# Attention and mixture of experts on one core: one transpose per group's shifts, the logits' maxima a step earlier, and small arithmetic of the norms on GpSimd

## What is computed

```python
mod = (silu(c) @ wmod).reshape(16, 6, 1, 128)          # sa, ca, ga, sb, cb, gb
h = layernorm(x, eps=1e-5) * (1 + ca) + sa
x = x + ga * attention(h)                              # 16 heads of 8, rope, causal
h = layernorm(x, eps=1e-5) * (1 + cb) + sb
x = x + gb * ffn(h)
# ffn: logits = h @ router.T; the 2 best of 8 experts per token;
#      shares = softmax over the two; out = sum of share * expert(h), hidden 512, gelu
```

## Time and profile before

| what | before |
|---|---|
| median of three runs | 526.88 us |
| the profiled execution, its own time | 525.71 us |
| its span, first to last instruction | 523.9 us |
| TensorE busy, share of the span | 455.6 us, 87% |
| VectorE busy | 385.0 us, 73% |
| ScalarE busy | 327.8 us, 63% |
| GpSimd busy | 329.0 us, 63% |
| granted TensorE clock, mean | 0.960 |

### The profile page before, as it was taken

One profiled execution on the slowest core, in us unless ns is written; L12 is line 12 of the kernel. 1 busy time (PEld: TensorE's weight loads), 2 busy tenths in 40 slices (PEclk: granted clock), 3 DMA queues, 4 the chain that ended last, 5 costly groups with the idle time before them and its releaser, 6 DMA issues.

```text
span 523.9 us, 12596 instructions
## 1 busy us (share of the span) xinstructions
PE 455.6 (87%) x3546; PEld 336.6 (64%) x3546; DVE 385.0 (73%) x1171; ACT 327.8 (63%) x896; POOL 329.0 (63%) x465
## 2 busy tenths in 40 slices
PE   4389999999999899989989999799789889999980
PEld 4255656665555555655656665389688788999970
DVE  4678898899999899999899899735336523434783
ACT  4666667656656556556566565677566557787860
POOL 3244465458858857957867958845656664444781
PEclk9689999999999999999999999899989789999995
DMA  4345655564664655664655862422212322223744
GB/s 120 101 129 150 135 152 152 140 182 140 184 177 135 180 143 162 195 175 126 188 135 146 172 155 80 132 73 64 72 52 66 88 73 67 69 67 106 226 135 140
DMA packets 77987, 67.88 MB, mean 130 GB/s; under 512 B 10916, under 2 KB 71592, under 8 KB 77921
## 3 DMA queue, kind: packets, MB, share of 16 engines
q1 hardware_dynamic: 71984, 57.18, 41.3%
q0 software_dynamic: 4320, 8.47, 5.0%
q10 hardware_dynamic: 1616, 1.44, 0.8%
HBM read 25.47 MB, written 12.05 MB: 72 GB/s over the span
## 4 chain that ended last, share of the span: by engine, by line
PE 38%; DVE 18%; issue 14%; POOL 13%; DMA 7%; ACT 5%; another core or an unknown queue 2%; SPq 2%; ACTq 1%; DVEq 0%; POOLq 0%
PE ps_sc L1637 8%; DVE maxima L1452 5%; PE ps_pv L1744 4%; PE misc L1627 4%; PE ps_max L1627 4%; PE misc L1790 4%; POOL sorted_rows L714 3%; POOL probs L764 3%; PE ps_sc L1715 3%; PE ps_max L1697 2%; POOL results L754 2%; DMA sorted_rows<-rows,slots 2%; ACT after_k L862 2%; PE ps_max L1618 1%
## 5 line engine op out<-in xcount | busy, mean ns | idle before, releaser
L1452 DVE TENSOR_REDUCE maxima<-ps_max 128x2 f32<-128x512 f32 (+1 forms) x192 | 130.1, 682 | 21.1 <-PE ps_max L1699 18.0
L930 ACT ACTIVATE probs<-ps_sc 128x512 f32<-128x512 f32 x192 | 109.8, 595 | 52.3 <-PE ps_sc L1715 40.8
L754 POOL DMA_INDIRECT results<-after_k,after_e x71 | 70.2, 988 | 63.5 <-DVE after_k L1149 46.0
L1715 PE MATMUL ps_sc<-q_diags,k_stacks 128*128 128x512 f32 x192 | 97.2, 508 | 5.7 <-ACT probs L930 3.3
L764 POOL TENSOR_SCALAR_AFFINE_SELECT probs<-probs 128x512 f32<-128x512 f32 x128 | 82.5, 652 | 24.5 <-ACT probs L930 23.2
L1637 PE MATMUL ps_sc<-wproj_s,after_k 128*128 x568 | 81.8, 289 | 1.8 <-ACT after_k L862 0.8
L1637 PEld LDWEIGHTS ps_sc<-wproj_s,after_k 128*128 128x128 f32 x568 | 72.2, 199 | 7.0 <-issue 4.7
L714 POOL DMA_INDIRECT sorted_rows<-rows,slots x64 | 65.4, 1021 | 14.5 <-issue 9.6
L1149 DVE SCALAR_TENSOR_TENSOR after_k<-ps_sc,after_e,after_k 128x128 f32<-128x128 f32 x71 | 24.8, 349 | 62.2 <-PE ps_sc L1637 32.3
L1697 PE MATMUL ps_max<-k_diags,q_stacks 128*128 128x512 f32 x128 | 61.2, 479 | 2.1 <-DVE maxima L1452 1.9
L1744 PE MATMUL ps_pv<-probs,v_wides 128*32 128x256 f32 (+1 forms) x1024 | 55.2, 333 | 3.6 <-POOL probs L764 3.5
(11 more groups left out here) (189 smaller groups left out, 920.8 us busy)
## 6 DMA issues: line engine op xcount, KB each, us to landing
k_diags<-k_stacks SPq DMA_DIRECT2D x64, 128.0 KB
q_diags<-q_stacks SPq DMA_DIRECT2D x64, 128.0 KB
gate_now<-gate_rows SPq DMA_DIRECT2D x16, 320.0 KB
after_e<-sorted_rows SPq DMA_DIRECT2D x71, 65.0 KB
k_stacks<-high SPq DMA_DIRECT2D x32, 128.0 KB
q_stacks<-high SPq DMA_DIRECT2D x30, 128.0 KB
x_in<-in_x SPq DMA_DIRECT2D x16, 128.0 KB, 2.8
k_stacks<-low SPq DMA_DIRECT2D x16, 128.0 KB
```

Source lines behind the costliest of these rows:

```text
L754: nc.gpsimd.indirect_dma_start(result_dram, bass.IndirectOffsetOnAxis(ap=row_in[m % RING][:, D + 1:D + 2].bitcast(U32), axis=0), y_out[m % ...
L930: nc.scalar.activation(probs[:, g % 2, c], ps_sc[u % 2][:], ACT.Exp, scale=SCALE).then_inc(S["exp_done"], 1)
L1452: nc.vector.tensor_reduce(to, of, AX, ALU.max).then_inc(S["max_done"], 1)
L1715: last = nc.tensor.matmul(ps_sc[u % 2][:].rearrange("p (w q) -> p w q", w=4), k_stack[(s.t + d) % 3][:, g, keys * P:(keys + 1) * P], q_dia ...
```

## The change

- **Shifts.** `shifts` now holds both query tiles side by side, 16 columns in the order part, head, tile. One transpose gives 16 rows of 128; ScalarE copies 16 x 128, and the DMA reads 16 rows of 128 in place of 8 rows of 256. 
- **Epsilon.** VectorE's 32 additions (L1050) go; GpSimd does them right ahead of its root, in slot 5 and slot 10. VectorE now waits ahead of the aggregation for the last reader of `moments`.
- **nmr.** VectorE's 14 instructions (L1546) go; GpSimd makes mean times rstd and then its negative behind the root in slot 10, each behind a wait for the one before, on 14 images.
- **Logits' maxima.** The four MAX8 of a routing step (slot 5) move to the end of the step before it (slot 11). The indices move from slot 7 to 5, `find_hot` from slot 8 to 7. The last pair of images, in the tile stage, stays as it was.
- The transpose of a bias in the prologue counts on another semaphore.

```diff
-        shifts = sb("shifts", [P, 2, TILES, P], F32R)
-        shift_t = [sb(f"shift_t{n}", [8, T], F32R) for n in range(2)]
+        shifts = sb("shifts", [P, 2, P], F32R)
+        shift_t = [sb(f"shift_t{n}", [8 * TILES, P], F32R) for n in range(2)]
...
                     if n == RESIDUAL_AT + 1 and s.has(-2):
+                        s.wait(pool, S["moments2_done"], -2, 2, 2)
+                        nc.gpsimd.tensor_scalar_add(var_eps2[:], moments2[:, :, 1], EPS).then_inc(S["eps2_done"], 1)
                         s.wait(pool, S["eps2_done"], -2, 1, 1)
...
                     if d and s.has(d):
+                        s.wait(pool, S["moments_done"], d, 2, 2)
+                        nc.gpsimd.tensor_scalar_add(var_eps[:], moments[:, :, 1], EPS).then_inc(S["eps_done"], 1)
                         s.wait(pool, S["eps_done"], d, 1, 1)
                         s.wait(pool, S["z_done"], d - 1, 2, 2)
                         nc.gpsimd.tensor_tensor(rstd[:], var_eps[:], half_s[:], ALU.pow).then_inc(S["rstd_done"], 1)
+                        if d == 3:
+                            s.wait(pool, S["rstd_done"], d, 1, 1)
+                            nc.gpsimd.tensor_tensor(var_eps[:], moments[:, :, 0], rstd[:], ALU.mult).then_inc(S["mean_scaled"], 1)
+                            s.wait(pool, S["mean_scaled"], 1, 1, 1)
+                            nc.gpsimd.tensor_scalar(nmr[:], var_eps[:], -1.0, None, ALU.mult).then_inc(S["nmr_done"], 1)
...
-                    nc.scalar.activation(shift_t[g % 2][:], misc[BANK[f"sh{g}"]][0:8, 0:T], ACT.Copy).then_inc(S["shift_out"], 1)
+                    nc.scalar.activation(shift_t[g % 2][:], misc[BANK[f"sh{g}"]][0:8 * TILES, 0:P], ACT.Copy).then_inc(S["shift_out"], 1)
...
                 s.wait(dve, S[sd], d, 2, 2)
+                s.wait(dve, S[rd], d - 1, 1, 1)
+                if d == 3 and s.t >= 0:
+                    dve.wait_ge(S["nmr_done"], s.t + 1)
                 for a in range(TILES):
                     nc.vector.bn_aggr(mo[:, a, :], st[:, a, :]).then_inc(S[md], 1)
-                s.wait(dve, S[md], d, 2, 2)
-                s.wait(dve, S[rd], d - 1, 1, 1)
-                nc.vector.tensor_scalar_add(ve[:], mo[:, :, 1], EPS).then_inc(S[ed], 1)
...
-                    v = shifts[:, g % 2, :, 0:8].rearrange("p a (f w) -> p a f w", f=2)
+                    v = shifts[:, g % 2, 0:8 * TILES].rearrange("p (f w a) -> p a f w", f=2, w=4)
...
                         if n == 5:
-                            find_top(s)
+                            find_at(s)
                         elif n == 7:
-                            find_at(s)
                             find_gap(s)
+                            find_hot(s)
                         elif n == 8:
-                            find_hot(s)
                             choose(s)
...
+                    if n == UNITS - 1 and s.t < B and Step(s.t + 1).routes():
+                        find_top(Step(s.t + 1))
...
-                    if n == 0 and s.t >= 0 and s.has(2):
-                        s.wait(dve, S["rstd_done"], 2, 1, 1)
-                        if s.t >= 1:
-                            dve.wait_ge(S["z_done"], 2 * (s.t + 2))
-                        nc.vector.scalar_tensor_tensor(out=nmr[:], in0=moments[:, :, 0], scalar=-1.0, in1=rstd[:],
-                                                       op0=ALU.mult, op1=ALU.mult).then_inc(S["nmr_done"], 1)
...
-                    for a in range(TILES):
-                        last = nc.tensor.transpose(bank[:, a * P:(a + 1) * P], shifts[:, g % 2, a, :].bitcast(F32), ident_s[:])
-                    last.then_inc(S["shift_tr"], 1)
+                    nc.tensor.transpose(bank[:, 0:P], shifts[:, g % 2].bitcast(F32), ident_s[:]).then_inc(S["shift_tr"], 1)
```

22 lines of the change are left out of this document (11 added, 11 removed).

## The result

| | before | after |
|---|---|---|
| median, 20 runs each, on one chip | 528.23 us | 525.88 us |
| ratio, with its 95% interval | | 0.9946 [0.9926, 0.9967] |
| the profiled execution, its own time | 525.71 us | 522.25 us |
| its span | 523.9 us | 519.9 us |
| TensorE / VectorE / GpSimd busy | 455.6 / 385.0 / 329.0 us | 447.9 / 368.3 / 344.3 us |

The ratio leaves out runs in a slower state, four of the change's 20, so it says a little more than the two medians, which are 2.4 us apart. By the ratio the change gains 0.54%, 2.9 us, where 4.8 us were forecast. Three more timings of the same change, on three other chips, gave 0.9967 [0.9941, 0.9993], 0.9974 [0.9942, 1.0005] and 0.9955 [0.9927, 0.9983], so 1.4 to 2.4 us there. The sign was right, the size about half.

The account below looks back on a forecast made before the run. TensorE was taken to bound plain steps, VectorE routing steps, GpSimd sorting steps from slot 3. Transposes -3.1, maxima -1.7, epsilon -2.3 and -1.2, additions +1.7 and +1.8 sum to -4.8 us: median 522.1 us, range 515 to 530.

Parts of the forecast that it names:

- GpSimd is the limit from slot 3 of a sorting step: Sorting and routing steps: GpSimd limits from there to slot 3 of the routing step behind; TensorE waits 0.66 us.
- I take 0.3 of the 0.84: Slot 3 of routing steps: three GpSimd additions make the sums 0.84 us late; 0.3 counted, 6 x 0.3 = +1.8 us.
- held instructions come free: Rival, routing steps: the low part slips ahead of GpSimd's masks, 5.4 us more gain, about 516.7 us; chance 0.15.
- near 20.0: Sign in the changed kernel's profile: routing steps near 20.0 us in place of 20.6.
- GpSimd becomes the bound: Rival, sorting and routing steps: all four GpSimd additions count in full, +4.9 us, about 531.8; chance 0.15.
- Transposes: Attention stage: 64 fewer on TensorE, 0.44 us a plain step, 0.22 a sorting step, nothing in routing steps; -3.1 us.
- Copy and DMA of the shifts: Attention stage: ScalarE's copy some 0.1 us shorter but hidden, DMA of 16 rows causes no wait; 0.
- Logits' maxima: Routing steps: four MAX8 leave VectorE's bound stretch for cover at the sorting step's end; -0.28 x 6 = -1.7 us.
- Epsilon on VectorE: Removing it wins 0.19 us each, two a routing step, -2.3 us; 0.2 a sorting step, -1.2 us.
- `nmr` on VectorE: Slot 0: removing it wins 0, since VectorE then waits 0.65 us for TensorE anyway.
- The additions on GpSimd: Attention stage: 0.2 us each plus 0.08 wait; +1.7 us ahead of slot 5's root, +1.8 us behind the mask.
- The rule of the Trainium skill: Each GpSimd instruction added can hold another on VectorE; by it the sum would lose the sorting steps' 1.2 us.

Follow-up runs that it names:

- no_norms: The changed kernel with epsilon and nmr both back on VectorE; ratio to the kernel before 1.0035.
- split_sort: nmr_back with both epsilons also back on VectorE in the sorting steps alone; ratio to the kernel before 0.9882.
- split_two: nmr_back with only the epsilon of slot 5 back on VectorE in sorting steps; ratio to the kernel before 0.9813, on another chip 0.9857.
- nmr_back: The changed kernel with nmr alone back on VectorE in slot 0, epsilon left on GpSimd; ratio to the kernel before 0.988, on another chip 0.9874.
- delay_only: no_norms with two unread additions on GpSimd ahead of the root of slot 10 in sorting steps; ratio to the kernel before 0.9949.
- before_third: The kernel before, unaltered, timed again beside the changed kernel on one more chip; ratio 1.0001.
- after_fourth: The changed kernel, unaltered, timed in the same call as before_third; ratio to the kernel before 0.9955.
- after_again: The changed kernel, unaltered, timed again on a chip of the faster kind; ratio to the kernel before 0.9967.
- after_third: The changed kernel, unaltered, timed beside nmr_back and split_two on one chip; ratio to the kernel before 0.9974.

## Why the prediction was wrong

**The step that failed first** is "GpSimd is the limit from slot 3 of a sorting step", with the terms put on it: "+0.28 x 6 = +1.7" for the epsilon of slot 5, and "I take 0.3 of the 0.84" for the three instructions behind the mask. It was read from step 7 alone. In the earlier trace rows the 0.91 us of waiting for a landing and the 0.66 us of TensorE belong together, and in step 9 neither is there: GpSimd then releases no sums with a wait. Such a step takes 18.85 us. With the change it takes 19.46: a longer step by 0.6, where the terms gave -0.14 (-0.22 - 0.2 + 0.28). The experiments give each term. One transpose wins nothing there (`no_norms` 18.93), nor does epsilon taken from VectorE (`split_sort` 18.92, `split_two` 18.97). The epsilon of slot 5 on GpSimd costs 0.2 (`split_two` 18.97, `nmr_back` 19.16, on different chips), near the 0.28. And the `nmr` pair costs another 0.3 (19.16 to 19.47), where the prediction had put its price on the routing step alone. The path was also another: not through the fourth DMA and its landing but straight, epsilon, root, DMAs and masks one behind the other up to the mask at 165.24, for which TensorE waits 0.88 us. The landing wait that was to be pushed back vanished instead (0 in steps 5 to 12 of the profiles after against 1 or 2 before), which returned some 0.5 to 1.6 us per execution and hid the mistake in step 7's own windows (19.81 to 19.46).

**Routing steps** were forecast to lose 0.36 each (-0.28 - 0.38 + 0.3), and lost 1.0. (By its own terms that is 20.26 us; the "near 20.0" among the signs leaves out the 0.3.) A part of it is the rival "held instructions come free", of which 0.15 was thought: `delay_only` shows 0.6 us of it without any work taken from VectorE. Another part is that the epsilons were priced too low: -0.38 a routing step, and 0.8 in `split_sort`, where the low part is held as before. The argument against the rival, that the rope sum is as late, was right too. At 0.37 us of delay the 0.6 us are there (20.05). At 0.91 us VectorE waits 0.55 and it is nearly gone (20.50). The rival's price was wrong in one more way: the low part does not fall to 0.4 but to 0.75 to 0.94, since it then runs beside the indirect DMA's issue (177.48 to 178.46) and ends 0.26 us behind it.

**The rival "GpSimd becomes the bound"** was at work at the same time, in the sorting steps and in front of the low part. It worked by place, not at the price of 0.7 us per product that was named. What was won in the routing step, 1.0 us, and lost in the sorting step, 0.6, leaves the usual pair 0.35 us shorter, with landing waits counted 0.5, where the terms gave 0.50. The sum of the pair's terms was right by luck.

**Where the total came short.** The second step that failed, and the one by which the number came short, is the count: "6 x" on every term of a pair, and four plain steps at 0.44. Here is what the terms give for each stretch of the table above, and what was measured:

| stretch | forecast | measured |
|---|---|---|
| plain steps | -1.8 us | -1.3 us |
| t = 4 | -0.4 | -0.5 |
| four pairs, t = 5 to 12 | -2.0 | -2.1 |
| t = 13 to 15, up to the last maxima | -0.6 | +0.4 |
| last maxima to last scores | 0 | +0.8 |
| behind the last scores | 0 | +1.1, not told from nothing |

Of the 3.0 us that are missing in these profiles, 1.0 lie in steps 13 to 15 and 0.5 in the plain steps; the other 1.9 lie behind the last maxima, and their cause stays open. The change wins nothing over steps 13 to 15. From VectorE's first `shifts` of one step to that of the next, step 13 takes 18.75 us before and 19.4 to 19.7 in the change, step 14 17.7 and 17.1: so step 13 loses some 0.8 us and step 14 wins 0.6. Why step 13 loses it was not looked into. Behind the last maxima the granted clock falls to 0.53 or lower in at least one window of 2 us in six of the seven profiles of the two kernels. That the loss there is the change's own was not shown, and one comparison speaks against it. With the clock falling alike, 0.77, 0.50 and 0.88 in three windows of `before_third` and 0.78, 0.50 and 0.86 in `after_fourth`, the stretch takes 12.57 and 12.67 us. Where the clock stayed at 1.00, in `after_again`, it takes 11.38; where it was at 0.50 for five windows, in `after_third`, 13.99.

The other terms, by their own steps:

- *Transposes*, -3.1 in all, of it -0.44 in each plain step: -0.44 in step 1, at most 0.05 in step 3, and +0.65 in step 4, for which nothing had been put. In the pairs 0.1 where 0.22 were forecast. The term took it that TensorE bounds a plain step and "all of it counts"; the step that it was read from, step 2, held a pause of 0.50 us, and with one transpose VectorE's low part is held there.
- *Copy and DMA of the shifts*, 0: the copy fell from 372 to 264 ns, and the score products show no new wait for it up to step 12. Right.
- *Logits' maxima*, -0.28 a pair: 0.26, by profiles on two chips of one kind. As far as that goes, right.
- *Epsilon on VectorE*, -0.38 and -0.2 a pair, less what GpSimd's delay costs: 0.8 in a routing step, nothing in a sorting step. What was not seen is that the same instruction, put on GpSimd, is the delay that frees the low part: with `nmr` on VectorE, the pair wins 1.58.
- *`nmr` on VectorE*, 0, and its price on GpSimd 0.3 a pair: going from `nmr_back` to the change costs 0.94 a pair (38.00 to 38.94), three times that. The 0.15 us that it saves on VectorE lay in a wait, as said; what it costs is the product and `slot_hot` held in slot 11 (1.0 us together, where `nmr_back` has 0.46 for the copy between them; the prediction had "slot 10 of routing steps ... 0"), the 0.88 us in front of the low part, and 0.3 in the sorting step.
- *The additions on GpSimd*, 0.2 + 0.08 each: 0.20 to 0.25 and 0.08 to 0.09. Right.
- *The rule of the Trainium skill*, page "GPSIMD Engine Reference", section "Specifications", that VectorE instructions with two SBUF inputs meet contention from GpSimd. The sentence built on it, that the sum would lose the 1.2 us of the sorting steps, falls short both ways: the product of 128 x 4 in the routing step was hit too (0.16 to 0.70), and `delay_only` shows that two more instructions on GpSimd can free one. A copy of 128 x 8, with one input, was held as well (0.16 to 0.62 us in `nmr_back`); in which mode it runs no run shows. The trace agrees with the rule's kind of instruction: rows from PSUM, as the maxima at 0.68 to 0.69, are as long beside GpSimd as without it.

## What to carry to other kernels

Before a term rests on a wait, look for the same wait in the other passes through the same loop and in a second profile: here 0.94 us of one sorting step stood for a limit that two of four steps of that profile, and three of four in two others, did not have, and a plain step with a pause of 0.50 us stood for all four. Where an instruction of one engine is held by another's, its length is a question of which of the two starts first, and a shift of some tenths of a microsecond can be worth more than the work that is moved; move the pieces one by one, since both halves together won 0.6 us a pair and each alone 1.1 and 1.6. And count a repeated gain only over those passes whose bound you have looked at, not over the last ones, where the pipeline drains.
